# A graph-network kernel with attention heads moved by way of memory: ten of a pair's sixteen heads instead of seven, and one group of four heads spent a slot later

## The reference

```python
for l in range(3):                                    # first network
    si, sj = x @ attn_w[l, :d], x @ attn_w[l, d:]
    scores = leaky(si[:, :, None] + sj[:, None, :] + attn_b[l])
    attn = softmax(where(mask, scores, -inf))         # mask: adjacency + identity
    h = layernorm(x + attn @ x, g1[l], beta1[l])
    x = layernorm(h + gelu(h @ W1[l] + b1[l]) @ W2[l] + b2[l], g2[l], beta2[l])
...
xh = heads of (x @ W_proj)                            # second network, 8 heads
scores = leaky(a_src[..., :, None] + a_dst[..., None, :] + b_att)
out = relu(softmax(where(A > 0, scores, NEG)) @ xh)
```

## Time and profile before

| | us |
|---|---|
| median of 3 runs | 2313.42 |
| lowest to highest | 2313.23 to 2313.54 |
| the profiled execution's own time | 2312.53 |
| its span, first to last instruction | 2310.8 |
| mean granted TensorE clock | 0.985 of full speed |

### The profile page before, as it was taken

The page is one execution under the profiler, slowest core; times in us unless marked ns, Lnnn a source line. Parts: engine busy times, 40 slices in busy tenths (PEclk is TensorE's granted clock), DMA queues, the critical chain, the costliest instruction groups (busy, mean ns, idle before and its releaser), DMA issues.

```text
span 2310.8 us, 32320 instructions
## 1 busy us (share of the span) xinstructions
PE 2213.7 (96%) x10501; PEld 1560.7 (68%) x10501; DVE 1809.3 (78%) x5722; ACT 1684.7 (73%) x3243; POOL 201.1 (9%) x200
## 2 busy tenths in 40 slices
PE   5999999999999999999999999999999999999976
PEld 3766767767766777676676667766776776777643
DVE  5566687878788788887788797887878877766777
ACT  2444468777877768777787778787787877888786
POOL 0010110010100110001100101000100011001100
PEclk9999999999999999999999999999999999999978
DMA  6011025333172242432353430632415322200111
GB/s 221 10 37 55 10 96 158 106 115 124 28 219 87 74 142 78 155 124 65 109 154 97 137 119 29 203 107 73 135 53 184 110 64 93 69 19 19 37 42 37
DMA packets 115874, 219.30 MB, mean 95 GB/s; under 512 B 7768, under 2 KB 57212, under 8 KB 110332
## 3 DMA queue, kind: packets, MB, share of 16 engines
q1 hardware_dynamic: 115708, 217.24, 29.8%
HBM read 164.52 MB, written 52.69 MB: 94 GB/s over the span
## 4 chain that ended last, share of the span: by engine, by line
PE 79%; DVE 13%; ACT 4%; issue 2%; POOL 1%; DMA 0%; DVEq 0%; POOLq 0%; ACTq 0%
PE ffn L1246 22%; PE av L1163 14%; PE ffn L1235 12%; PE av L1235 12%; PE pT L1146 9%; PE av L1187 4%; PE av L1222 2%; DVE prob L778 2%; DVE prob L769 1%; ACT xs L553 1%; POOL rstd L470 1%; DVE lone L730 1%; PE trow L1125 1%; PE av L1273 1%; PE trow L1273 1%
## 5 line engine op out<-in xcount | busy, mean ns | idle before, releaser
L1246 PE MATMUL ffn<-w_sb,G 128*128 128x256 f32 x3072 | 740.5, 381 | 0.0
L1246 PEld LDWEIGHTS ffn<-w_sb,G 128*128 128x128 f32 x3072 | 560.8, 191 | 90.2 <-issue 24.3
L778 DVE CUSTOM_DVE_ANT_0 prob<-trow,mask 128x512 f32<-128x512 f32 x676 | 439.0, 685 | 34.3 <-PE trow L1125 19.5
L1146 PEld LDWEIGHTS pT<-ident,prob 128*128 128x128 f32 x2032 | 256.4, 144 | 147.6 <-issue 101.5
L1235 PE MATMUL ffn<-hT,w_sb 128*128 128x512 f32 x768 | 355.0, 595 | 0.9 <-issue 0.9
L1235 PE MATMUL av<-hT,w_sb 128*128 128x512 f32 x768 | 353.8, 593 | 0.0
L470 POOL TENSOR_TENSOR rstd<-veps,mhalf 128x4 f32<-128x4 f32 x127 | 167.2, 1317 | 2071.9 <-DVE veps L713 2071.9
L513 ACT ACTIVATE prob<-prob,s 128x512 f32<-128x512 f32 x484 | 331.5, 715 | 2.4 <-DVE nm L785 1.8
L1146 PE MATMUL pT<-ident,prob 128*128 128x128 f32 x2032 | 312.3, 278 | 19.8 <-DVE prob L841 7.5
L519 ACT ACTIVATE prob<-prob,nm 128x512 f32<-128x512 f32 x448 | 317.6, 712 | 0.0
L1163 PE MATMUL av<-xs,prob 128*128 128x257 f32 x1024 | 244.3, 380 | 3.9 <-ACT prob L524 3.9
(11 more groups left out here) (154 smaller groups left out, 2727.2 us busy)
## 6 DMA issues: line engine op xcount, KB each, us to landing
w_sb<-in_L_gnn_W SPq DMA_DIRECT2D x48, 1024.0 KB, 8.4
blocks_dram<-blocks SPq DMA_DIRECT2D x168, 256.0 KB, 4.2
prob<-blocks_dram SPq DMA_DIRECT2D x42, 1024.0 KB, 4.8
trow<-rows_dram SPq DMA_DIRECT2D x127, 256.0 KB, 3.2
adj_sb<-in_adj SPq DMA_DIRECT2D x16, 1024.0 KB, 7.0
xin<-in_x SPq DMA_DIRECT2D x16, 512.0 KB, 6.2
x0r<-in_x SPq DMA_DIRECT2D x16, 512.0 KB, 5.8
out<-o SPq DMA_DIRECT2D x15, 512.0 KB, 3.2
```

Of the source, the lines that this page charges most:

```text
L778: return v.tensor_tensor_reduce(out=out_[:, t, :], in0=targets, in1=mask[:, t, :], scale=1.0, scalar=LEAST, op0=ALU.add, op1=ALU.max, accu ...
L1146: last = te.transpose(pT[bank][:, j * P:(j + 1) * P], src[:, t, j * P:(j + 1) * P], ident[:])
L1246: last = te.matmul(ffn[part][:, at:at + D], G[:, f, t * P:(t + 1) * P], w2_sb[:, g // 2 % STAGES, f, :], start=f == 0, stop=f == FT - 1)
```

## The change

Three more heads of each pair are moved by way of memory: 6, 9 and 14. The order is changed around them:

- slot 3: heads 6 (ahead of the attention on VectorE) and 8 (behind it) are moved; TensorE turns head 7 in its first product instead of head 6, and none later.
- slot 4: heads 9 (ahead) and 10 (behind) are moved; TensorE turns only head 11, between pieces. Nothing is turned in its first product, and a fifth piece of the second product is done before the attention.
- slot 0: head 14 is moved (ahead); TensorE turns head 15 in its first product, and none later.
- heads 8 to 11 are spent in slot 5, behind step f = 1 of the first product, and transposed back behind f = 3, instead of at the end of slot 4.
- in slots 3 and 0 the four heads are spent at the slot's end, and `transpose_state` comes after the pieces of the last loop's t = 3 instead of t = 1; in slot 4 it comes after t = 2.

```diff
-BY_BLOCKS = (1, 2, 4, 5, 8, 10, 13)
-AHEAD = (2, 4)
+BY_BLOCKS = (1, 2, 4, 5, 6, 8, 9, 10, 13, 14)
+AHEAD = (0, 2, 3, 4)
...
 def turned_ahead(g):
-    return [q for q in turned(g)[1:2] if moved(q) and g % SLOTS in AHEAD]
+    return [q for q in turned(g) if moved(q)][:1] if g % SLOTS in AHEAD else []
 def turned_behind(g):
-    return [q for q in turned(g)[1:] if moved(q) and q not in turned_ahead(g)]
+    return [q for q in turned(g) if moved(q)][len(turned_ahead(g)):]
+def turned_first(g):
+    return [q for q in turned(g)[:2] if not moved(q)][:1]
+def states_behind(place):
+    return {1: 3, 2: 2}.get(place, 1)
+def spent_later(g):
+    p, k = g // SLOTS, g % SLOTS
+    return side_by_side(turned(g - 1))[1] if k == SLOTS - 1 and p < PAIRS - 1 else None
...
 (ScalarE)
                     else:
-                        for q in heads[:1]:
+                        for q in turned_first(g):
                             turned_out(q, f - T)
+                    if f == 1 and spent_later(g) is not None:
+                        head_rows(spent_later(g))
...
-                    if t == 0 and place == 1:
-                        head_rows(four)
-                    if t == 1:
+                    if t == states_behind(place):
                         for dt in range(DT):
                             transposed(dt, l2)
...
                 for q in new[1:2]:
-                    if place == 2:
+                    if place in (1, 2) and spent_later(g + 1) is None:
                         head_rows(four)
...
 (TensorE)
+                more = 1 if heads and not turned_first(g) else 0
...
                     first_product(g, f)
+                    if f == 1 and spent_later(g) is not None:
+                        attend_heads(spent_later(g))
+                    if f == 3 and spent_later(g) is not None:
+                        heads_back(spent_later(g))
                     if f >= T:
-                        for q in heads[:1]:
+                        for q in turned_first(g):
                             turn(q, f - T)
-                for t in range(T):
-                    piece(t)
-                attention(s2, l2, g + 1, lambda i: piece(4 + i))
+                pieces(T + more)
+                attention(s2, l2, g + 1, lambda i: pieces(1))
...
                     if begin is not None:
                         project(begin, t)
-                    piece(10 + t)
-                    if t == 0 and place == 1:
-                        attend_heads(four)
-                    if t == 1:
+                    pieces(1)
+                    if t == states_behind(place):
                         for dt in range(DT):
                             transpose_state(s2, dt)
-                    if t == 2 and place == 1:
-                        heads_back(four)
-                if place == 2:
+                if place in (1, 2) and spent_later(g + 1) is None:
                     attend_heads(four)
-                piece(14)
+                pieces(1)
                 if begin is not None:
                     targets_in(begin)
-                if place == 2:
+                if place in (1, 2) and spent_later(g + 1) is None:
                     heads_back(four)
-                piece(15)
+                pieces(1 - more)
```

More of the change, by code:

```diff
@@ L623, in _ @@
                     for q in heads[1:2]:
-                        if not moved(q):
+                        if not moved(q) and q not in turned_first(g):
                             turned_out(q, t)
@@ L1309, in _, with pieces @@
                 begin = begun(g)
-                def piece(n):
-                    second_product(g, l, n)
+                order = iter(range(4 * T))
+                more = 1 if heads and not turned_first(g) else 0
+                def pieces(count):
+                    for _ in range(count):
+                        second_product(g, l, next(order))
                 for f in range(FT):
@@ L1331, in _ @@
                         state_in(begin, t - T + DT)
-                    piece(6 + t)
+                    pieces(1)
                 if place == 0:
```

## The result

The changed kernel takes 2336.64 us (median of 4 runs, 2335.59 to 2339.26) against 2313.32 us of the kernel before (2312.81 to 2313.54, 4 runs). The ratio is 1.0105, with an interval from 1.0089 to 1.0121. The forecast was 2321 with a range to 2331: the sign was right, and 15.6 us are missing from the sum. The profiled execution took 2336.38, with a span of 2334.5 against 2310.8, 23.7 more.

What follows compares the result with a forecast made beforehand. VectorE's chain was taken to bound slots 3 and 4, TensorE slot 5. Terms -3.35 + 4.20 + 0.1 + 0.4 give +1.35 us a round, +8.1 over six rounds: 2321 us, range 2307 to 2331.

Steps and rivals of the forecast that it cites:

- slots 3 and 4 as one chain: From slot 3's last attention product, VectorE's chain reaches slot 5's start in 59.4 us, winning 3.35 a round.
- four heads in slot 5: Slot 5 is TensorE's alone, so it grows by all of the four heads' 4.20 us, to 48.6.
- landing of head 10: In slot 5, head 10's data land 16.7 us after the last product, TensorE needs them at 16.8: cost 0.1.
- slot 0: Head 14's block turn delays VectorE's fold, so product 2 and the state's transposes wait: 0.4 us lost a round.
- Cost 0 to 0.5; I take 0.1: The charge a round in slot 5 for the four heads waiting on head 10's landing, 4.8 us after issue.
- I see nothing large in flight then: Argument against head 10 landing late in slot 5: no large transfer beside its read; no size of its own.
- late move: Rival: head 10 lands later than 16.8 us behind the product; with 1.3 more, 2329 us; chance 0.17.
- Part 2: Three more block turns on VectorE, 2.31 us each; through slots 3 and 4 this gives 3.35 us won a round.
- VectorE's tail does not hold slot 5: Rival: TensorE's tail of 11.0 to 12.0 us sets slot 4's end, not 13.35: 2307 to 2313 us; chance 0.17.
- TensorE sets everything: Rival: all 5.23 us saved a round come through, 2282; without slots 0 and 4's losses about 2267; chance 0.08.
- VectorE counts in full: Rival: all 18 added block turns of 2.31 us lengthen the time, 41.6 more, 2355 us; chance 0.03.

Runs made afterwards that it cites:

- e1_fill: Changed kernel with two unread TensorE products put in each idle, before slot 4's target row and slot 5's step 0: 2331.23 us, ratio 1.0084.
- e8_fill_later: Changed kernel with unread products in both idles, and heads 8 to 11 spent behind f = 3, back behind f = 5: 2323.47 us, ratio 1.0052.
- e4: Kernel before with only heads 8 to 11 spent in slot 5, behind f = 1 and back behind f = 3: 2311.67 us, ratio 0.9999.
- e5: Changed kernel with VectorE's mask work of slot 3 done at the end of slot 4: 2313.20 us, ratio 1.0004.
- e6: Kernel before with only head 6 moved and slot 3's new order: 2312.28 us, ratio 0.9996.
- e3: Kernel before with only head 14 moved and slot 0's new order: 2318.31 us, ratio 1.0026.
- e7: e3 with slot 0's statistics of the first network's output put behind the attention on VectorE, GpSimd's order following: 2298.57 us, ratio 0.9944.
- e12: e7 with the mask work made in slot 4 and slot 4's state transposes after t = 2: 2301.78 us, ratio 0.9945.
- e2: Changed kernel with heads 8 to 11 spent in slot 5 behind f = 3, back behind f = 5: 2333.08 us, ratio 1.0093.
- e9: e2 with slot 4's first fold put ahead of graph_out on VectorE: 2316.36 us, ratio 1.0018.

## Why the prediction was right in sign and too low

Terms a round, us. The measured column has means over six rounds of the profiles. It takes the clock's share as the changed kernel's slots less e1_fill's (slot 5) and e8_fill_later's (slot 4), the landing as e1_fill's slot 5 less e8_fill_later's, and the chain with e8_fill_later's slot 4.

| term | predicted | measured |
|---|---|---|
| slots 3 and 4 as one chain | -3.35 | -3.27 (89.53 less 92.80) |
| four heads in slot 5 | +4.20 | +4.28 (e8), +4.20 (e4) |
| landing of head 10 | +0.1 (0 to 0.5) | +1.09 |
| slot 0 | +0.4 (0.2 to 0.6) | +0.80 |
| half clock, slot 4 and slot 5 | none | +0.62 and +0.42 |
| sum | +1.35 | +3.94 |

Six rounds of 3.94 are 23.7, and the two profiled spans differ by 23.7. So two steps carry most of the miss of 15.6 us: the half clock behind a new idle, which stood in no term (1.04 a round), and the landing (1.0 too small); slot 0 adds 0.4. The sign was not luck: with clock and landing both put right the kernel is still slower (e8, ratio 1.0052).

- **Chain of slots 3 and 4: right.** Its stations were each met within 0.1, its length was 59.48, and e5 and e6 show that it is VectorE's: one shortens it without touching TensorE's work, the other shortens TensorE's work and nothing changes.
- **What the -3.35 hides.** It is the difference between 4.2 us won by sending the four heads to slot 5, which slot 5 pays back in full, and a loss. Against e4, which sends them there and moves no head more, slots 3 and 4 are 0.94 longer (89.53 less 88.59). So moving heads 6 and 9 wins nothing over slots 3 and 4 together, and the whole 23.7 us are the price of the three moves and their order, as e4 takes as long as the kernel before.
- **Slot 5 pays the four in full: right**, by e4.
- **The landing: the step "Cost 0 to 0.5; I take 0.1" was mis-sized.** Two things add up: the read was issued 6.26 and not 6.0 behind the block turn, and it landed 5.65 and not 4.8 later (5.65 to 6.13 in the six rounds). The 4.8 is the median of 42 moves, of which 37 had no store close behind. The trace of before had the other kind too, 6.11 to 6.21. The prediction's "I see nothing large in flight then" was wrong: the output's store and the mask load follow on the same queue within 0.9 us. The rival of the late move had it, "each us is six".
- **The clock: a step that is missing.** The prediction lets TensorE wait some 3 us in slot 4 and 1.3 to 2.4 at slot 5's start, and Part 2 prices these waits at their own length. That the clock can fall behind them was in no case, and neither bound of the range had it. The trace of before had a hint, in a window of the first pair's slot 3, where no head is turned. TensorE stands idle for 2.46 there, the clock falls behind it, and the window's mean is 0.96. In the changed kernel the same work, with the same idle, takes 40.25 at 1.00:

```profile
164.97:206.69 41.72, 39.26 (x157) 28.26 (x156) 27.45 (x91) 16.53 (x24) 4.31 (x3) 0.96 0.00 0
```

- **Slot 0: right in kind, mis-sized.** The wait at product 2 was 1.84 (1.95), that at the transposes 0.24 (up to 0.4). The sum of the two less 1.74 is 0.34; the slot grew by 0.80, in e3 by 0.79. The new order of the rest is not the difference: e7 has it, and its slot 0 is 44.55, the 46.30 of before less 1.74. It lies in the waits themselves, which cost more than their idle. Counted from the slot's start, product 2 begins at 28.50 in e3 and at 26.50 in e7, 2.0 later for an idle of 1.84; the state's transposes are 2.5 later, for 2.09 of idle in all.
- **The rivals.** "VectorE's tail does not hold slot 5" is out: TensorE waits 2.28 at f = 0. "TensorE sets everything" and "VectorE counts in full" are out by e6: one would have been 10 faster, the other 14 slower. The late move was true, at 1.1 of the 1.3 that it assumed, beside the forecast and not in its place. In "TensorE sets everything" the 2267 is a slip: 0.9 and 2.1 more a round are 18 us, which gives 2264.

## What to carry to other kernels

Price a new idle of TensorE at its length and at the slower clock that may follow, and look for both at the place where the work resumes. Where two engines are level within a few us, find out on which chain a removed instruction lies before spending another engine's time on it. Here 96 transposes less in slot 3 gave nothing. VectorE's mask work, moved one slot on in the changed kernel, gave 23 us, and its statistics, moved behind the attention in the same slot, gave 19 (e7 against e3, by the ratios). But the same move of the masks gave 0.07 a round in e12, where another wait stood right behind. And a transfer needs its slack against the landings beside the same neighbours, not against the median of all.

## What the chip showed that was not expected

- TensorE's granted clock fell to half behind idles of 2.42 and 2.28 us in a stretch that is otherwise busy, in four rounds of six; in the others, behind the same 2.28, it stayed at full (1.00 in 1057.50 to 1059.50). Behind the idle of 1.97 in the second pair's slot 0 it fell in the profiles of the changed kernel, e2, e3, e8 and e9, and not in those of the kernel before, e1, e4, e5 and e6. In slots 4 and 5 of e4_four_later and e6_head6, whose idles were shorter (1.09 and 1.69 at most), it did not fall. What decides this is open.
- The same small instruction of GpSimd, `shift`, 128x4, takes 0.20 us in most places and 1.27 in some, and the timelines show which. It takes 1.26 or 1.27 wherever it starts together with an element-wise operation of VectorE on two inputs of 128x1024 (`plus_bias` or the start of `graph_sum`), 17 times in the kernel before, 11 in the changed one and 10 in e7_net_behind; it ends 0.06 behind that operation each time. Nowhere else does it take more than 0.60, and beside a block turn it takes 0.20, 30 times in the changed kernel. That is why slot 4's slow shift of before (1.26) is fast in the changed kernel: head 10's block turn (1047.71) now stands beside it. In slot 0 it stays slow, which delays the normalising that the state's transposes wait for. The timelines of GpSimd and of VectorE in the changed kernel:

```profile
869.73 1.27 POOL L491 TENSOR_TENSOR shift<-nmean,rstd 128x4 f32<-128x4 f32 x1
...
1047.71 0.20 POOL L491 TENSOR_TENSOR shift<-nmean,rstd 128x4 f32<-128x4 f32 x1
```

```profile
869.72 1.22 DVE L900 TENSOR_TENSOR xs<-xs,bias_row 128x1024 f32<-128x1024 f32 x1
```
